# Mirrored attention tiles turned by VectorE blocks and a trip through DRAM instead of by TensorE

## What is computed

```python
h = jnp.maximum(_layernorm(x, axis=-1), 0.0)
# _L2_gnn_ref(h, adj, weight, bias)
h = x @ weight
h_norm = h / jnp.maximum(jnp.linalg.norm(h, axis=1, keepdims=True), NORM_EPS)
sim = h_norm @ h_norm.T
attn = jax.nn.softmax(sim / TAU + jnp.log(adj + EPS), axis=1)
out = attn @ h + bias
```

## Time and profile before

| | us |
|---|---|
| median of 3 runs (1366.87 to 1370.17) | 1367.85 |
| the profiled execution | 1367.61 |
| its span | 1365.8 |
| loop, 575 to 1158 us of the span | 583 |

### The profile page before, as it was taken

The page is one execution under the profiler, slowest core; times in us unless marked ns, Lnnn a source line. Parts: engine busy times, 40 slices in busy tenths (PEclk is TensorE's granted clock), DMA queues, the critical chain, the costliest instruction groups (busy, mean ns, idle before and its releaser), DMA issues.

```text
span 1365.8 us, 26517 instructions
## 1 busy us (share of the span) xinstructions
PE 1312.9 (96%) x9996; PEld 995.4 (73%) x9996; DVE 983.8 (72%) x1958; ACT 558.6 (41%) x1336; POOL 215.2 (16%) x289
## 2 busy tenths in 40 slices
PE   4899999989999999999999999999999998899998
PEld 3788888864555555567777777777777776788887
DVE  6898998958355555577778788768777888876642
ACT  3586544726122222344444544544545444311111
POOL 2000000012322222210000000000000000465443
PEclk9999999999999999999999999999999999999999
DMA  9999999720111220300021110111101100551500
GB/s 239 261 346 300 392 393 374 293 87 17 60 57 55 63 62 1 109 24 32 24 65 30 32 32 24 32 32 34 34 28 32 29 12 23 141 132 40 147 25 24
DMA packets 82574, 141.19 MB, mean 103 GB/s; under 512 B 8720, under 2 KB 50704, under 8 KB 82448
## 3 DMA queue, kind: packets, MB, share of 16 engines
q1 hardware_dynamic: 79376, 137.39, 32.0%
q10 hardware_dynamic: 3072, 2.10, 0.5%
HBM read 118.49 MB, written 20.97 MB: 102 GB/s over the span
## 4 chain that ended last, share of the span: by engine, by line
PE 84%; DVE 7%; POOL 2%; SPq 2%; issue 2%; ACT 1%; DMA 1%; ACTq 0%; DVEq 0%
PE ps L1645 12%; PE ps L1732 10%; PE ps L1631 8%; PE ps L1532 8%; PE ps L1533 8%; PE ps L1632 8%; PE ps L1494 7%; PE ps L1495 7%; PE ps L1662 4%; PE ps L1681 4%; PE ps L1693 4%; DVE ring L730 1%; SPq L399 1%; DMA acc<-in_adj 1%; SPq L404 1%
## 5 line engine op out<-in xcount | busy, mean ns | idle before, releaser
L1494 PE MATMUL ps<-val_hi,ring 128*128 128x257 f16 x1024 | 226.4, 274 | 0.0
L1495 PE MATMUL ps<-val_lo,ring 128*128 128x256 f16 x1024 | 226.3, 273 | 0.0
L1532 PE MATMUL ps<-ring,acc 128*128 128x512 fp8e4 x512 | 194.1, 379 | 5.4 <-DVE acc L867 5.3
L1645 PE MATMUL ps<-hnt 128*128 128x512 f16 (+3 forms) x864 | 197.5, 365 | 0.0
L1533 PE MATMUL ps<-ring,acc 128*128 128x512 fp8e4 x512 | 194.0, 379 | 0.0
L1414 ACT ACTIVATE ring<-ring 128x512 f16<-128x512 f32 (+2 forms) x133 | 79.4, 597 | 231.1 <-DVE ring L1002 231.0
L730 DVE STREAM_TRANSPOSE ring<-acc 128x1024 uint8<-128x1024 uint8 x128 | 151.4, 1218 | 29.1 <-DMA acc<-in_adj 29.0
L1002 DVE SCALAR_TENSOR_TENSOR ring<-ring,ps 128x512 f32<-128x512 fp8e4 (+2 forms) x133 | 85.7, 644 | 97.1 <-PE ps L1681 96.5
L1631 PE MATMUL ps<-val_hi,hs 128*128 128x257 f16 x534 | 145.8, 273 | 2.1 <-DVE hs L983 2.1
L1662 PE MATMUL ps<-val_hi,hs 128*128 128x257 f16 x534 | 145.8, 273 | 0.0
L1632 PE MATMUL ps<-val_lo,hs 128*128 128x256 f16 x534 | 145.6, 273 | 0.0
(11 more groups left out here) (229 smaller groups left out, 2334.4 us busy)
## 6 DMA issues: line engine op xcount, KB each, us to landing
acc<-in_adj SPq DMA_DIRECT2D x256, 256.0 KB, 8.0
at_dram<-ring SPq DMA_DIRECT2D x32, 512.0 KB, 9.0
ring<-at_dram SPq DMA_DIRECT2D x64, 256.0 KB, 2.9
ring<-at_dram SPq DMA_DIRECT2D x24, 512.0 KB, 3.9
ring<-at_dram SPq DMA_DIRECT2D x9, 1024.0 KB, 9.4
val_lo<-at_dram SPq DMA_DIRECT2D x4, 1024.0 KB, 10.5
xs<-in_x SPq DMA_DIRECT2D x12, 256.0 KB, 11.8
val_hi<-at_dram SPq DMA_DIRECT2D x3, 1024.0 KB, 8.9
```

Source lines behind the costliest of these rows:

```text
L1494: nc.tensor.matmul(ps[:, k % 8, 0:D + 1], lhs, val_hi0[:, t, 0:D + 1], start=(t == 0), stop=False)
L1495: last = nc.tensor.matmul(ps[:, k % 8, 0:D], lhs, val_lo0[:, t, :], start=False, stop=(t == NB - 1))
L1532: nc.tensor.matmul(ps[:, bank + c, :], g_hi[:, t, c * P:(c + 1) * P], src, start=(t == 0), stop=False)
L1645: last = nc.tensor.matmul(ps[:, 4 + n % 2, k:GW], hnt[:, a, c, j * P:(j + 1) * P], hnt[:, b, c, g * GW + k:(g + 1) * GW], start=(c == 0 an ...
```

## The change

The transposes of the 112 outer tiles leave PE. DVE transposes the tile in 32x32 blocks (`turn`), two tiles side by side in one buffer; one DMA writes the pair to DRAM and four DMAs, one for each 32 partitions, read it back so that the blocks land where a full transpose puts them. The mirror of an outer step n is weighed and summed three steps later (`LAG = 3`), and `mirror_weights` reads the tile from `back` in SBUF instead of bank 6. The inner steps keep their PE transposes and their place. `mirror_low` goes from DVE to POOL. So that it can be a plain subtraction, the scale PSC goes into the exponential's tile: ACT now takes the exponential in place in PSUM and then copies it with the scale into `e_t`, which has two buffers instead of three. The `adj` tiles of layer four get other homes and load times, and four of the preparation steps of DVE stand later in the loop. Some semaphores are merged.

```diff
-        e_t = [ring[:, 6 * N + i * 1024:6 * N + (i + 1) * 1024].bitcast(F32) for i in range(3)]
+        e_t = [ring[:, 6 * N + i * 1024:6 * N + (i + 1) * 1024].bitcast(F32) for i in range(2)]
+        turned = [ring[:, a:a + 2048].bitcast(F32) for a in (N + 2048, 6 * N + 2048)]
+        back = [ring[:, a:a + 2048].bitcast(F32) for a in (7 * N + 2048, 7 * N)]
...
+        LAG = 3
+        def mirrors_at(n):
+            return ([n - LAG] if 0 <= n - LAG < NS and outer[n - LAG] else []) + ([n] if n < NS and inner[n] else [])
+        mirror_order = [o for n in range(NS + LAG) for o in mirrors_at(n)]
+        place = {o: m for m, o in enumerate(mirror_order)}
...
-            PREP[NB + 17 + r] = ("d5", "d5", r)
-            PREP[NB + 21 + r] = ("d7", "a12", r)
+            PREP[opens[4] + 12 + r] = ("d5", "d5", r)
+            PREP[opens[5] + 7 + r] = ("d7", "a12", r)
...
+            def write_pair(u):
+                sp.wait_ge(sem["turned"], 2 * u + 2)
+                sp.dma_start(turned_dram[u % 4], turned[u % 2]).then_inc(sem["written"], 16)
+            def read_pair(u):
+                sp.wait_ge(sem["written"], 16 * (u + 1))
+                if u >= 2:
+                    sp.wait_ge(sem["p2_done"], place[outer_steps[2 * u - 3]] + 1)
+                for b in range(4):
+                    sp.dma_start(back[u % 2][32 * b:32 * b + 32, :].rearrange("p (a e) -> p a e", a=4),
+                                 turned_q[u % 4, b]).then_inc(back_loaded[u % 2], 16)
...
+                if n == NB // 2:
+                    sp.wait_ge(sem["hnt_ready"], NB)
+                    load_raw(sp, 0, "22")
+                if n == opens[4] + LAG + 1:
...
+                    load_raw(sp, 0, "12")
...
+            def mirror_low(n):
+                m, k = place[n], mirror_blocks(n)[0] * P
+                pool.wait_ge(sem["hi2_done"], m + 1)
+                since(pool, sem["pv2_done"], m - 1)
+                nc.gpsimd.tensor_tensor(lo2[m % 2][:, k:GW], p2t[m % 2][:, k:GW], hi2[m % 2][:, k:GW],
+                                        ALU.subtract).then_inc(sem["lo2_done"], 1)
...
+            def turn(n):
+                m = n_outer[n]
+                dve.wait_ge(sem["exp_done"], n + 1)
+                since(dve, sem["written"], 16 * (m // 2 - 1))
+                nc.vector.transpose(turned[m // 2 % 2].rearrange("p (b j s q) -> p s q b j", b=4, s=2, j=32)[:, m % 2],
+                                    e_t[n % 2].rearrange("p (q b i) -> p q b i", q=GB, b=4)).then_inc(sem["turned"], 1)
...
+                    dve.wait_ge(back_loaded[o // 2 % 2], 64 * (o // 4 + 1))
+                    nc.vector.scalar_tensor_tensor(out.rearrange("p (q j) -> p q j", q=GB),
+                                                   chunk2[c % 3][:, :, r * P:(r + 1) * P], EDGE * ATTN_EPS,
+                                                   back[o // 2 % 2].rearrange("p (j s q) -> p s q j", s=2, q=GB)[:, o % 2],
+                                                   ALU.add, ALU.mult).then_inc(sem["p2_done"], 1)
...
-                nc.scalar.activation(e_t[n % 3][:, k:GW], ps[:, 4 + n % 2, k:GW], ACT.Exp, scale=1.0 / VSC ** 2).then_inc(sem["exp_done"], 1)
+                nc.scalar.activation(ps[:, 4 + n % 2, k:GW], ps[:, 4 + n % 2, k:GW], ACT.Exp, scale=1.0 / VSC ** 2).then_inc(sem["exp_raw"], 1)
...
+                act.wait_ge(sem["exp_raw"], n + 1)
+                nc.scalar.activation(e_t[n % 2][:, k:GW], ps[:, 4 + n % 2, k:GW], ACT.Copy, scale=PSC).then_inc(sem["exp_done"], 1)
```

More of the change, by code:

```diff
@@ L77, in gnn_kernel @@
         c2_loaded = [ctx.enter_context(nc.semaphore(f"c2_loaded{i}")) for i in range(3)]
+        back_loaded = [ctx.enter_context(nc.semaphore(f"back_loaded{i}")) for i in range(2)]
         raw_loaded = {k: ctx.enter_context(nc.semaphore(f"raw{k}_loaded")) for k in ("11", "22", "12", "21")}
@@ L284, in gnn_kernel @@
         inner = [g > 0 and j < (g + 1) * GB and j % GB < GB - 1 for g, j in order]
-        mirrored = [a or b for a, b in zip(outer, inner)]
-        n_mirrored = [sum(mirrored[:n]) for n in range(NS + 1)]
         n_outer = [sum(outer[:n]) for n in range(NS + 1)]
+        n_inner = [sum(inner[:n]) for n in range(NS + 1)]
+        LAG = 3
[3 more added lines that the diff above has]
+        place = {o: m for m, o in enumerate(mirror_order)}
+        NM = len(mirror_order)
         def first_block(n):
@@ L640, in _ @@
                     root_norm(late_at["project2"][n])
-            for g in range(NG):
-                pool.wait_ge(sem["var3_ready"], g + 1)
-                nc.gpsimd.tensor_tensor(rstd4[g % 2], ve4[g % 2], half[:, 0:GB], ALU.pow).then_inc(sem["rstd3_ready"], 1)
+                for g, i in tail_at(n):
+                    if i == 9:
+                        root_var3(g)
+                for o in mirrors_at(n + 1):
+                    mirror_low(o)
+            root_var3(NG - 2)
+            root_var3(NG - 1)
             for n in range(NB // 2):
@@ L1201, in _ @@
                     weights(n + 1)
-                if mirrored[n]:
-                    mirror_low(n)
+                if n + 1 < NS and outer[n + 1]:
+                    turn(n + 1)
                 if n + 1 < NS:
                     weights_low(n + 1)
-                if n > 0 and outer[n - 1]:
-                    add_mirror(n - 1)
+                for o in mirrors_at(n - 1):
+                    if outer[o]:
+                        add_mirror(o)
+                if n == NS - 1:
+                    for o in mirrors_at(n):
+                        if outer[o]:
+                            add_mirror(o)
                 if n in PREP:
@@ L1226, in _ @@
                     group_tail(g, i)
-                if n + 1 < NS and mirrored[n + 1]:
-                    mirror_weights(n + 1)
+                if n + 1 < NS:
+                    for o in mirrors_at(n + 1):
+                        mirror_weights(o)
             group_tail(NG - 2, 9)
@@ L1238, in _ @@
             group_tail(NG - 1, 9)
-            dve.wait_ge(sem["t_done"], n_mirrored[NS])
+            dve.wait_ge(sem["lo2_done"], NM)
             dif2(0)
@@ L1459, in _ @@
                     group_tail(g, i)
-                if n + 1 < NS and mirrored[n + 1]:
-                    mirror_high(n + 1)
+                if n + 1 < NS:
+                    for o in mirrors_at(n + 1):
+                        mirror_high(o)
             for i in range(TAIL):
@@ L1710, in _ @@
                 weighted(n)
-                if n + 1 < NS and mirrored[n + 1]:
+                if n + 1 < NS and inner[n + 1]:
                     mirror(n + 1)
-                if mirrored[n]:
-                    mirror_weighted(n)
+                for o in mirrors_at(n):
+                    mirror_weighted(o)
             FACTORS = (("a11", 1, 0), ("d5", "right", 1), ("a22", 0, 2), ("d2", "left", 3), ("d1", "fifth", 4), ("a21", 2, 5), ("a12", 3, 6))
```

191 lines of the change are left out of this document (97 added, 94 removed).

## The result

The changed kernel takes 1390.47 us (median of 4 runs, 1389.46 to 1395.27), the kernel before 1369.01 beside it (4 runs, 1366.87 to 1371.53). The ratio is 1.0163, with a 95% interval of 1.0132 to 1.0194: the change makes the kernel slower by 1.6%, where 1337 us had been forecast. The profiled execution took 1395.27 us, the longest of the four, with a span of 1393.5.

The account below looks back on a forecast made before the run. TensorE was taken to bound the loop. From 1367.6 us: -49.3 for transposes, +9 for the GpSimd lock, +5 for group starts, +4 for 1 MB loads gave 1336.3, rounded 1337; own range 1320 to 1350, with rival 1 1320 to 1407.

Parts of the forecast that it names:

- What bounds the kernel: In the attention loop TensorE is the bound, busy 573 of 583 us, at 4.37 us per outer step.
- TensorE's saving: 112 outer steps lose their four transposes, 0.44 us each: -49.3 us, leaving a step of 3.93 us.
- for each of the two the price is between 0 and a doubling: Extra VectorE cost of 32-byte steps in `turn` and `mirror_weights`: 0 to 0.53 us each, taken as 0.
- Rival 1: 32-byte steps cost VectorE a doubling in both operations, +1.06 us a step: 1405 us; chance 0.25.
- the sign that I gave for being wrong: The forecast is wrong if VectorE is busy over 95% of the attention loop.
- rival 2: Only one of VectorE's two 32-byte-step operations doubles: 1365 to 1385 us, put at 1375; chance 0.14.
- The lock and GpSimd: GpSimd's low-half subtraction and VectorE wait for each other, 0 to 0.7 us per step: +9 us in all.
- The round trip: A pair's write to DRAM and read back takes 8.5 us, covered by 10.7 us, so it costs nothing.
- Rival 3: The DRAM trip outlasts its cover, at 11.7 us, 1 us for each of 56 pairs: 1393 us; chance 0.09.
- The raw loads: Two 1 MB loads inside the loop among the pair DMAs cost +2 us each, +4 together.
- group starts and the dense end: Seven group starts cost 0.7 us each, +5; preparation moved to the loop's end was counted within the lock's +9.

Follow-up runs that it names:

- e10: e3 with GpSimd's mirrored low half computed for one column of each tile only, so the sums are wrong: 1342.8 us, 0.9819 of the kernel before.
- e13: e10 plus the 1 MB loads in quarters and the mirror's sums alternating between two PSUM banks away from group starts: 1333.9 us, 0.9733 of the kernel before.
- e3: The changed kernel with `turn` writing and `mirror_weights` reading side by side instead of 32 bytes apart (wrong elements): 1363.3 us, 0.9959 of the kernel before.
- e5: The changed kernel with the mirrored low half back on VectorE instead of GpSimd: 1414.7 us, 1.0337 of the kernel before.
- e6: e3 with the mirrored low half back on VectorE instead of GpSimd: 1362.0 us, 0.9946 of the kernel before.
- e1: The changed kernel with only `turn` writing side by side instead of 32 bytes apart (wrong elements): 1388.8 us, 1.0148 of the kernel before.
- e7: The kernel before with only the mirrored low half moved to GpSimd as a plain subtraction, its scale left out: 1377.4 us, 1.0061 of the kernel before.
- e8: e3 with the two 1 MB loads inside the loop cut into quarters of 256 KB, one every second step: 1361.0 us, 0.9942 of the kernel before.

## Why the prediction was wrong

**What bounds the kernel, and TensorE's saving: right.** The 448 transposes went, and TensorE's busy time in the loop fell by 33 us (573 to 540). That it isn't 49 is partly how busy time is counted: of a product 0.27 us long with 0.11 to the next start, the last 0.16 count as busy at every pause, and there are many pauses now. Where nothing holds TensorE the forecast step appears: in e10, from 660 to 675 us, its scores start at 662.98, 666.91 and 670.85, so 3.93 and 3.94 us apart. In e13 the scores of the loop run from 573.1 to 1114.6, 541.5 us, against 580.2 before and 530.9 by the -49.3.

**The step that failed: "for each of the two the price is between 0 and a doubling ... I take 0".** It measures 0.40 us for each, three quarters of the upper end of 0.53 (for which the prediction gives no working; a doubling of its 0.61 would be 0.61). The reason I gave for 0 was that operations of bytes and of four-byte elements cost the same for one element; that says that the rate does not hang on the width of an element, not that it does not hang on the distance between two. The row that did have such a distance, the memset of GpSimd, showed 0.24 against 0.12, and I set it aside as another engine's. It was the only row on the question, and it pointed the right way. The two steps were worth 27 us together (e3 against the change): more than the whole excess over the time before (21.5). Nearly all of it is the reading step; with the low half on VectorE, where nothing hides the writing one, the two are worth 53 us (e5 against e6).

The Trainium skill's rule on SBUF's lines of 16 bytes (Advanced Engine Details and Errata, SBUF Cachelines), named in the prediction as speaking against the change, holds here: with 32 bytes from element to element every access is to a line of its own, and the traces put 0.8 ns on each, in reading and in writing alike. No run here tried another distance, so where the price begins is not shown.

**Rival 1 had the cost, at three quarters of its price, but not the way to the time.** It said 1405 for 0.53 us twice and that it decides once VectorE needs more than 4.37 us a step. In the step shown above VectorE needs 5.27, where it had 4.98; the steps are cheaper than it said, the lock is dearer (`weights_low` 1.15 instead of 0.61), and this step has 1.21 us of side work where the mean has 0.80. But rival 1 made the loop as long as VectorE's work and 10 us more. With the measured 0.40 its sum is 457 - 81 + 68 + 90 + 47 = 581, so a loop of 591 and a time of 1376. VectorE's work was 558 and the loop 608: 50 us in which VectorE waited are in no rival. So 1390.5 came near 1405 in part by luck, and the sign that I gave for being wrong, VectorE busy over 95% of the loop, did not show (92%); the other one did, `turn` and `mirror_weights` at 1.1 us instead of 0.69. In what counted for the time the outcome is nearer to rival 2, one of the two: the reading step alone makes 25 of the 27 us.

**The lock and GpSimd: the mechanism right, the size wrong.** GpSimd's subtraction takes 1.17 us (1.3 to 1.46 expected), and stretches `weights_low` by 0.20 us on the mean in the changed kernel, 0.26 to 0.31 in e3 and e1, within the 0 to 0.7 that I gave. What I priced was only VectorE's load, +9. The low half holds 20.5 us (e3 against e10). The likely reason is that it also stands on the path of the mirror, so that bank 7 comes free only behind ScalarE and GpSimd. e7 points the same way without any of the other edits: 8.4 us where a load-only view would have given a gain or nothing. The lock's term was 11 us too small.

**The round trip: right.** SP's rows of the changed kernel, and the groups of DMAs by kind (KB each, us from issue to landing), as the earlier trace rows:

```profile
862.84 0.34 SPq L503 DMA_DIRECT2D turned_dram<-ring  x1
863.23 0.43 SPq L487 DMA_DIRECT2D ring<-at_dram  x1
865.84 1.74 SPq L511 DMA_DIRECT2D ring<-turned_dram  x4
```

```profile
turned_dram<-ring SPq DMA_DIRECT2D x56, 512.0 KB, 2.9
ring<-turned_dram SPq DMA_DIRECT2D x224, 128.0 KB, 2.8
```

The reads are issued 3.0 us behind the write, the last of the four begins some 1.3 later and lands 2.8 after that: 7.1 us, where 8.5 was expected and 10.7 left. VectorE waited for `back` six times in the whole loop, 12.4 us. Rival 3 did not come about.

**The raw loads: about right.** The longest of these six waits, 4.57 us at 1033, lies behind a 1 MB load, as foreseen. In e8, with the loads in quarters, the time is 2 us lower, within the noise, where the prediction had +4. The fall of the clock behind that wait was not foreseen; it is below.

**What is left, group starts and the dense end among it: too small by 11 to 16 us.** e10 is 15.5 us over the sum without the lock (1327.3), e13 still 11 over its own (1323). Of these, 6 are located at the dense end. I had set the dense end's preparation inside the lock's term and the single bank nowhere.

So the 54 us between the sum of 1336.3 and 1390.5 are 27 for the steps, 11 for the lock and its chain, and 16 that are left over, waits at the dense end and for the bank among them. The split holds for this order of taking things away (the steps, then the low half); in another order the steps weigh more. The first decided the sign: without it the kernel would have been 0.4% faster than before (e3), still 26 us short of the forecast.

## What to carry to other kernels

Before an access pattern is put into the busiest loop, look at how far two neighbouring elements lie apart, and if nothing in the profile has that distance on that engine, price it at the nearest row that has it, even if it is another engine's. Work given to a second engine is priced by its place on the path and not only by what it frees: a low half that took 0.69 us became 1.17, made the neighbour's operation longer, and lost 8 us where hardly anything else was changed. When an engine gets rid of 0.4 us in every step and the time doesn't move, look in the timeline for what the next operation waits for: here ScalarE's tile and GpSimd's subtraction had hidden exactly that much. And a sum of an engine's work is a lower end for the time, not the time: VectorE, 92% busy, stood idle for 50 us of the loop.

## What the hardware showed that I had not expected

A block transpose of f32 takes 701 ns for 512 elements a partition, written side by side: the rate of a plain f32 operation of that size (680 to 691 ns in the same kernels). A third free dimension cost `tensor_tensor` nothing: 679 ns, against 680 for `scalar_tensor_tensor` with two.

The clock. The prediction put no clock effect into the sum. Windows of the changed kernel around the stall of 1033, and TensorE's rows behind it:

```profile
1030.00:1040.00 10.00, 5.53 (x39) 3.55 (x37) 5.36 (x11) 3.27 (x7) 1.61 (x2) 0.99 0.82 236
1040.00:1050.00 10.00, 9.00 (x47) 5.66 (x48) 10.00 (x15) 6.26 (x12) 3.25 (x3) 0.67 0.57 180
```

```profile
1041.00 0.39 PE L1699 MATMUL ps<-val_hi,ring 128*128 128x257 f16 x1 [5.47 <-POOL ring L683]
...
1043.54 2.77 PE L1713 MATMUL ps<-hnt 128*128 128x512 f16 x6
1046.10 0.42 PE L1699 MATMUL ps<-val_hi,hs 128*128 128x257 f16 x1
```

TensorE stood idle for 5.47 us and came back at the 1.2 GHz level: twelve products and the six of the scores took 1046.10 - 1041.00 = 5.10 us, where 1.32 + 1.29 = 2.61 is the cost at 2.4 GHz. The granted clock of those 10 us is 0.67. So one late DMA cost TensorE 5.5 us of waiting and 2.5 on top at that place; the quarters of e8 gain 2 us of time against e3. In e8, with the load in quarters, the granted clock from 1000 to 1070 us is 0.98, in e3 it is 0.95.
